# Second routing's logits from the old row and the activations, and the chain's steps in new slots

## The reference, cut to what matters

```
x = x + 0.5 * ffn(layernorm(x))          # 4096 rows of 128
x = x + attn(layernorm(x))               # a gated linear recurrence over time, then a gated FFN, then Wo
x = x + 0.5 * ffn(layernorm(x))

ffn(x):  gate_logits = x @ Wg            # 128 -> 12 experts
         topw, sel = top_k(gate_logits, 3); softmax over the three
         h = gelu(x @ Wup[e] + bup[e])   # 128 -> 512
         y = h @ Wdown[e] + bdown[e]     # 512 -> 128
         sum of the three chosen experts' y by weight
attn(x): u = silu(x@Wg + bg) * (x@Wi + bi); y = scan of u over time; y = Cp*y + Dp*u; normalise
         y = (silu(y@Wfg + bfg) * (y@Wfu + bfu)) @ Wfd + bfd; return y @ Wo + bo
```

## Time and profile before

| | us |
|---|---|
| median of 3 runs | 632.81 (632.74 to 634.7) |
| profiled execution, whole time | 633.43 |
| its span, first to last instruction | 631.7 |
| busy: TensorE / ScalarE / GpSimd / VectorE | 564.4 / 419.8 / 418.0 / 348.7 |
| first expert matmul | 43.6 |
| passes 1, 2, 3 begin (first up) | 171.5 / 320.0 / 473.3 |

### The profile page before, as it was taken

The page is one execution under the profiler, slowest core; times in us unless marked ns, Lnnn a source line. Parts: engine busy times, 40 slices in busy tenths (PEclk is TensorE's granted clock), DMA queues, the critical chain, the costliest instruction groups (busy, mean ns, idle before and its releaser), DMA issues.

```text
span 631.7 us, 17884 instructions
## 1 busy us (share of the span) xinstructions
PE 564.4 (89%) x4591; PEld 529.5 (84%) x4591; DVE 348.7 (55%) x1636; ACT 419.8 (66%) x1280; POOL 418.0 (66%) x432
## 2 busy tenths in 40 slices
PE   8469999999699999999999899999979999989505
PEld 7358999999699889879899789899979999989502
DVE  5983365371014688987727589888743532232206
ACT  2547686686366787887668688877657766656204
POOL 1137777777767775556677777066666777777774
PEclk9769999999799999999999999999999999999957
DMA  7577776789598786466478967466568888765137
GB/s 214 180 190 236 211 196 202 218 205 275 156 288 255 215 240 178 138 188 189 135 215 255 275 212 206 148 187 183 160 175 249 217 281 251 215 194 156 49 119 244
DMA packets 121847, 127.90 MB, mean 202 GB/s; under 512 B 17178, under 2 KB 84561, under 8 KB 121749
## 3 DMA queue, kind: packets, MB, share of 16 engines
q1 hardware_dynamic: 106452, 99.52, 53.2%
q0 software_dynamic: 12992, 26.11, 14.8%
q10 hardware_dynamic: 2304, 1.11, 0.6%
HBM read 96.62 MB, written 30.79 MB: 202 GB/s over the span
## 4 chain that ended last, share of the span: by engine, by line
PE 54%; DMA 13%; POOL 12%; DVE 10%; issue 8%; ACT 1%; SPq 0%; DVEq 0%; POOLq 0%; ACTq 0%
PE ps L931 20%; PE ps L944 20%; POOL YG L739 6%; DMA YG<-ys,SY 4%; POOL yk L750 3%; PE ps L799 3%; DMA xl<-xn,SG 3%; PE ps L825 2%; POOL xs L723 2%; PE ps L901 2%; DMA yk<-Ys,row 2%; DMA xs<-XN,SX 2%; PE ps L891 1%; DMA ys<-Ys 1%; DVE YG L1563 1%
## 5 line engine op out<-in xcount | busy, mean ns | idle before, releaser
L1097 ACT ACTIVATE hT<-ps,BU 128x128 f32<-128x128 f32 x944 | 269.4, 371 | 109.3 <-PE ps L931 106.7
L931 PE MATMUL ps<-xT,WU 128*128 128x128 f32 x1888 | 253.8, 278 | 4.2 <-ACT hT L1097 2.3
L944 PE MATMUL ps<-WD,hT 128*128 x1888 | 252.4, 277 | 4.8 <-DVE Ys L1635 3.7
L931 PEld LDWEIGHTS ps<-xT,WU 128*128 128x128 f32 x1888 | 233.4, 194 | 13.9 <-issue 13.9
L944 PEld LDWEIGHTS ps<-WD,hT 128*128 128x128 f32 x1888 | 231.7, 193 | 6.9 <-issue 6.8
L723 POOL DMA_INDIRECT xs<-XN,SX x144 | 144.5, 1004 | 87.6 <-issue 66.2
L739 POOL DMA_INDIRECT YG<-ys,SY x144 | 150.1, 1042 | 48.5 <-issue 40.6
L1635 DVE TENSOR_TENSOR Ys<-ps,BD 128x128 f32<-128x128 f32 x236 | 67.5, 289 | 193.4 <-PE ps L944 182.7
L708 POOL DMA_INDIRECT xl<-xn,SG x59 | 59.7, 1011 | 30.4 <-issue 14.0
L750 POOL DMA_INDIRECT yk<-Ys,row x59 | 59.0, 1000 | 18.0 <-issue 13.2
L1074 ACT ACTIVATE xT<-ps 128x512 f32<-128x512 f32 (+1 forms) x55 | 32.6, 593 | 6.6 <-PE ps L901 2.9
(11 more groups left out here) (255 smaller groups left out, 540.1 us busy)
## 6 DMA issues: line engine op xcount, KB each, us to landing
WU<-in_L_ffn_Wup_dram SPq DMA_DIRECT2D x236, 256.0 KB
ys<-Ys SPq DMA_DIRECT2D x42, 256.0 KB
xl<-xs SPq DMA_DIRECT2D x118, 66.0 KB, 3.0
xl<-xs SPq DMA_DIRECT2D x59, 64.0 KB, 1.9
WD<-in_L_ffn_Wdown_dram SPq DMA_DIRECT2D x12, 256.0 KB, 4.9
WD<-yk SPq DMA_DIRECT2D x4, 768.0 KB, 7.2
xs<-XN,SX POOLq DMA_INDIRECT x144
YG<-ys,SY POOLq DMA_INDIRECT x144
```

Source lines behind the costliest of these rows:

```text
L931: x = e.matmul(HB[i % 2][:, c * P:(c + 1) * P], WU[i % NW][:, c * P:(c + 1) * P], xT[m % 2][:, j * P:(j + 1) * P], start=True, stop=True)
L944: x = e.matmul(YB[i % 2][:, 0:D], hT[i % 3][:, c * P:(c + 1) * P], WDf[:, bass.ds(r + c * P, P)], start=(c == 0), stop=(c == C - 1))
L1097: x = e.activation(hT[i % 3][:, c * P:(c + 1) * P], HB[i % 2][:, c * P:(c + 1) * P], ACT.Gelu, bias=BU[:, bass.ds(b + c, 1)])
```

## The change

For the second routing the logits of the new row are made of three parts. The new row is x + y + bias, where y = tg times wfo. Its product with wgc is (old normalised row x wgc) x deviation of the old row, plus tg x (wfo wgc), plus (bias x wgc). G1 makes the first part from sT, which A1 has turned already, and adds the third; A7 makes the second part from tg right after its own products; L on VectorE adds them (lgn) and goes on as before. The step T, its copy and the product of the new row with wgc go, in CHAIN alone (pass 0's ROUTE keeps them). S1 adds a reciprocal (sd). W2 and W3, in pass 0, make wgk = [wfo wgc, bias wgc]; `bo` is loaded once more as a column. Nearly all slots of CHAIN are new, the first table steps A0 to A2 of pass 2 come two slots earlier, FETCHED has nothing for tiles 0 and 1, `load_rows` for the next pass comes one tile earlier, and in first() the aggregates and part of the deviation move between the chosen() steps.

```diff
-BIAS = [("V", "B3", 3), ("PA", "W0", 3), ("PAV", "W1", 5), ("S", "W1", 7)]
+BIAS = [("V", "B3", 3), ("PA", "W0", 3), ("PAV", "W1", 5), ("S", "W1", 7), ("PVA", "W2", 7), ("PV", "W3", 9)]
 CHAIN = [
-    ("V", "G0", (10, 17, 25, 30, 10, 17, 24, 30)),
-    ("V", "G2", (14, 20, 27, 34, 14, 20, 26, 32)),
-    ("V", "S1", (15, 21, 28, 36, 15, 20, 27, 33)),
-    ("A", "G", (17, 23, 29, 38, 17, 22, 28, 35)),
-    ("PA", "A1", (18, 24, 31, 39, 18, 23, 30, 36)),
-    ("PA", "A2", (18, 25, 34, 40, 18, 24, 33, 39)),
-    ("V", "C1", (18, 26, 35, 42, 18, 25, 33, 40)),
...
-    ("PV", "A7", (31, 38, 44, 52, 28, 36, 44, 50)),
-    ("PA", "T", (32, 39, 45, 53, 30, 38, 45, 51)),
-    ("V", "N", (32, 39, 44, 52, 30, 39, 45, 50)),
-    ("V", "N'", (33, 41, 44, 53, 32, 40, 45, 50)),
-    ("PV", "L", (33, 40, 47, 53, 32, 39, 46, 52)),
-    ("A", "N", (35, 42, 46, 54, 33, 41, 47, 53)),
-    ("PVG", "K", (35, 41, 49, 55, 35, 41, 48, 54)),
+    ("V", "G0", (9, 15, 21, 27, 11, 17, 21, 28)),
+    ("V", "G2", (14, 19, 25, 30, 14, 19, 25, 30)),
+    ("V", "S1", (15, 19, 26, 31, 15, 19, 25, 31)),
+    ("A", "G", (16, 21, 27, 32, 17, 21, 27, 33)),
+    ("PA", "A1", (17, 22, 28, 34, 18, 22, 29, 35)),
+    ("PA", "A2", (17, 23, 29, 36, 18, 23, 31, 37)),
+    ("P", "G1", (17, 23, 29, 37, 18, 23, 32, 37)),
+    ("V", "G1", (17, 23, 28, 42, 21, 23, 32, 47)),
+    ("V", "C1", (17, 23, 29, 36, 18, 23, 33, 37)),
...
+    ("PV", "A7", (31, 37, 44, 50, 29, 36, 43, 47)),
+    ("V", "N", (32, 40, 45, 50, 32, 39, 43, 47)),
+    ("V", "N'", (34, 40, 45, 50, 33, 39, 44, 49)),
+    ("V", "L", (33, 38, 44, 52, 30, 36, 45, 48)),
+    ("A", "N", (35, 41, 47, 53, 35, 41, 46, 53)),
+    ("PVG", "K", (35, 41, 46, 55, 32, 40, 47, 54)),
 ]
-TABLES_AT = ((34, 38), (50, 63), (51, 64))
+TABLES_AT = ((34, 38), (50, 63), (49, 64))
-FETCHED = tuple(min(K * NT, 6 + (13 * k) // 25) for k in range(NTL))
+FETCHED = tuple(min(K * NT, 6 + (13 * k) // 25) if k > 1 else 0 for k in range(NTL))
...
-                if n + 1 < NPH and k in (NTL - 3, NTL - 2):
-                    load_rows(NG * (n + 1) + k - (NTL - 3))
+                if n + 1 < NPH and k in (NTL - 4, NTL - 3):
+                    load_rows(NG * (n + 1) + k - (NTL - 4))
...
+                elif kind == "G1":
+                    e.wait_ge(s_e1, c)
+                    old = bank(step)
+                    for j in range(4):
+                        i = e.matmul(old[:, j * E:(j + 1) * E], sT[q][:, j * P:(j + 1) * P], wgc[:], start=True, stop=True)
+                    i.then_inc(s_g1, 1)
...
+                    new = bank(step, 1)
+                    for j in range(4):
+                        i = e.matmul(new[:, j * E:(j + 1) * E], tg[q][:, j * P:(j + 1) * P], wgk[:, 0:E], start=True, stop=True)
+                    i.then_inc(s_lg, 1)
...
+                    if p:
+                        new = psum[USED[("A7", h, q, p)][1][0]]
+                        e.wait_ge(s_dv, dv.n)
+                        e.tensor_tensor(lgn[:], new[:, 0:4 * E].rearrange("p (t e) -> p t e", e=E), lgo[q][:], ALU.add
+                                        ).then_inc(s_d2, 1)
...
+                    dv.on(e.reciprocal(sd[q][:], nr[q][:]))
+                elif kind == "G1":
+                    old = ps[0]
...
+                    e.tensor_tensor(
+                        lgo[q][:], old[:, 0:4 * E].rearrange("p (t e) -> p t e", e=E),
+                        sd[q][:, :].rearrange("p (t o) -> p t o", o=1).to_broadcast([P, 4, E]), ALU.mult).then_inc(s_d1, 1)
+                    e.wait_ge(s_d1, c)
+                    dv.on(e.tensor_tensor(
+                        lgo[q][:], lgo[q][:], wgk[:, E:2 * E].rearrange("p (o e) -> p o e", o=1).to_broadcast([P, 4, E]), ALU.add))
...
                 stats(0)
                 stats(1)
-                for q in range(NQ):
-                    chosen(q)
-                    if q + 2 < NQ:
-                        stats(q + 2)
+                stats(2)
+                chosen(0)
+                stats(3)
+                spread(0, NT // 2)
+                chosen(1)
+                spread(NT // 2, NT)
...
```

More of the change, by code:

```diff
@@ L343, in macaron_kernel @@
         BO3 = sb("BO3", [3, D], BF16)
-        wfdT, wfo = sb("wfdT", [P, D]), sb("wfo", [P, D])
+        wfdT, wfo, woT, bT = (sb(n, [P, D]) for n in ("wfdT", "wfo", "woT", "bT"))
+        wgk = sb("wgk", [P, 2 * E])
+        sd = [sb(f"sd{c}", [P, 4]) for c in range(NQ)]
+        lgo = [sb(f"lgo{c}", [P, 4, E]) for c in range(NQ)]
+        lgn = sb("lgn", [P, 4, E])
         sT, tg, ag = ([sb(f"{n}{c}", [P, 512]) for c in range(NQ)] for n in ("sT", "tg", "ag"))
@@ L425, in macaron_kernel @@
             "s_t4", "s_e4", "s_g5", "s_i5", "s_a5", "s_u5", "s_wp", "s_wt", "s_wo", "s_wb", "s_p7", "s_X"))
+        s_q2, s_q2c, s_q3, s_q3c, s_g1, s_d1, s_d2 = (sem(n) for n in ("s_q2", "s_q2c", "s_q3", "s_q3c", "s_g1", "s_d1", "s_d2"))
         s_fin, s_out, s_fs, s_fp, s_fe = (sem(n) for n in ("s_fin", "s_out", "s_fs", "s_fp", "s_fe"))
@@ L882, in side @@
                              skip_group_check=True).then_inc(s_wo, 1)
+                elif kind == "G1":
[4 more added lines that the diff above has]
+                    i.then_inc(s_g1, 1)
+                elif kind == "W2":
+                    w2 = bank(step)
+                    e.matmul(w2[:, 0:D], wat["Wo"][:], wfdT[:], start=True, stop=True)
+                    e.matmul(w2[:, D:D + 1], wat["Wo"][:], vec["bfd"][:, 0:1], start=True, stop=True,
+                             skip_group_check=True).then_inc(s_q2, 1)
+                elif kind == "W3":
+                    e.wait_ge(s_q2c, 2)
+                    w3 = bank(step)
+                    e.matmul(w3[:, 0:E], woT[:], wgc[:], start=True, stop=True)
+                    e.matmul(w3[:, E:2 * E], bT[:], wgc[:], start=True, stop=True, skip_group_check=True).then_inc(s_q3, 1)
                 elif kind == "A7":
                     e.wait_ge(s_u5, c)
+                    e.wait_ge(s_q3c, 1)
                     e.wait_ge(s_wb, 2)
@@ L1051, in side @@
                     e.activation(wfo[:], ps[0][:, 0:D], ACT.Copy, scale=0.5).then_inc(s_wb, 1)
+                elif kind == "W2":
+                    e.wait_ge(s_q2c, 1)
+                    e.activation(woT[:], ps[0][:, 0:D], ACT.Copy, scale=0.5).then_inc(s_q2c, 1)
                 elif kind == "TO":
@@ L1226, in side @@
                 elif kind == "L":
-                    lg = ps[0]
                     v = V[h][:, 4 * q:4 * q + 4, :]
                     e.wait_ge(s_lg, r)
+                    if p:
[3 more added lines that the diff above has]
+                                        ).then_inc(s_d2, 1)
+                        e.wait_ge(s_d2, c)
+                        lg = [lgn[:, j, :] for j in range(4)]
+                    else:
+                        lg = [ps[0][:, j * E:(j + 1) * E] for j in range(4)]
                     for j in range(4):
-                        i = e.max(v[:, j, :], lg[:, j * E:(j + 1) * E])
+                        i = e.max(v[:, j, :], lg[j])
                     dv.on(i)
@@ L1234, in side @@
                     for j in range(4):
[L1235 removed]
+                        i = e.max_index(IX[q][:, j, :], v[:, j, :], lg[j])
                     dv.on(i)
@@ L1288, in side @@
                     e.wait_ge(s_c1, 2 * c)
+                    e.wait_ge(s_g1, c)
                     dv.on(e.tensor_tensor_scan(sT[q][:], vec["A"][:, 0:1].to_broadcast([P, 512]), tg[q][:], 0.0,
@@ L1324, in side @@
                             e.wait_ge(s_bp, 2 * n + 2)
+                elif kind == "W2":
+                    e.wait_ge(s_q2, 1)
+                    e.tensor_tensor(bT[:], ps[0][:, D:D + 1].to_broadcast([P, D]), vec["bo"][:, 0:1].to_broadcast([P, D]), ALU.add
+                                    ).then_inc(s_q2c, 1)
+                elif kind == "W3":
+                    e.wait_ge(s_q3, 1)
+                    e.tensor_copy(wgk[:], ps[0][:, 0:2 * E]).then_inc(s_q3c, 1)
                 elif kind == "B3":
@@ L1466, in stats, with spread @@
                         dv.on(e.bn_stats(st16[:, 4 * q + j, :], X[:, 4 * q + j, :]))
+                def spread(a, b):
+                    e.wait_ge(s_dv, dv.n)
+                    for t in range(a, b):
+                        i = e.bn_aggr(mv16[:, t, :], st16[:, t, :])
+                    dv.on(i)
+                    e.wait_ge(s_dv, dv.n)
                 def chosen(q):
@@ L1482, in first @@
                 stats(1)
-                for q in range(NQ):
-                    chosen(q)
-                    if q + 2 < NQ:
-                        stats(q + 2)
+                stats(2)
[4 more added lines that the diff above has]
+                spread(NT // 2, NT)
+                dv.on(e.tensor_scalar(v16[:], mv16[:, :, 1], 1e-5, None, ALU.add))
+                e.wait_ge(s_dv, dv.n)
+                dv.on(e.tensor_scalar(nr16[:].bitcast(I32), v16[:].bitcast(I32), -0.5, RSQRT_SEED, ALU.mult, ALU.add))
+                e.wait_ge(s_dv, dv.n)
```

(11 more changed lines are left out.)

33 lines of the change are left out of this document (10 added, 23 removed), and 18 rows, old and new, of the table CHAIN.

## The result

The changed kernel is slower: median 640.0 us (637.72 to 644.75, four runs) against 633.75 us (632.74 to 634.72, four runs) of the kernel before on the same chip, ratio 1.0089, 95% interval 1.0054 to 1.0123 (the quotient of the two medians, 1.0099, lies in it; the sums below go by the ratio, +5.6 us). The forecast was 628.2 us with a range up to 633.3. The profiled execution took 641.01 us, its span 638.9. In the changed kernel an up product is L960, a down product L973, VectorE's output copy Ys L1703, G1's product L895, A7's new product L921.

A forecast was written before the change was run, and what follows sets the result against it. TensorE was taken to bound passes 1 and 2, GpSimd pass 3 from its start. Terms -1.5 + 3.0 - 0.9 - 2.3 - 3.0 = -4.7 us gave a median of 628.2 us, range 624 to 633.3.

The forecast's parts named there:

- The start: In first(), before pass 0: the counts' operation starts earlier and GpSimd's first gather moves with it, -1.5 us (bounds 0 and 1.6).
- TensorE per chunk: Passes 1 and 2: T and L go, G1 and A7's second half come, +0.38 us per chunk, +3.0 us for eight.
- rival E: Short products' weight loads hide behind neighbours, so a group costs only its streaming; eight chunks change by -3.1, 622 us; chance 0.02.
- The idle term: TensorE in passes 1 and 2: 2.4 us of waits go, 1.5 new ones come; net -0.9 us, bounds -4 and +8.4.
- K of the last chunk: Pass 2, slot 54: L and tables come earlier, so VectorE's K can go at about 461.1; -2.3 us, bounds 0 and -2.5.
- The turn: Pass 2 to 3: GpSimd's 3.28 us gap, a wait for the last ys store, goes; -3.0 us, bounds -1.0 and -3.3.
- its price of nothing: Turn to pass 3: TensorE's 2.88 us wait for rows should mostly go, worth nothing at the end as TensorE leads GpSimd.
- D: VectorE waits at G0 of chunk 2, slot 21, for gathers and holds TensorE, 8.4 us in two passes; 637.4 us; chance 0.09.
- "Wrong" signs: Profile signs against the forecast, among them gather waits, TensorE idle above 8 us in passes 1 and 2, GpSimd waiting for Ys.
- "Waits DVE from YG gathers": Sign against the forecast: VectorE waits of several us for gathers at G0 or G2.

The follow-up runs named there:

- the run with the start alone: Kernel before with only the new order of the first table in first(): ratio 0.9958 (0.9938 to 0.9979), -2.7 us.
- The doubled group: Changed kernel with G1's eight short product instructions issued twice per chunk: 1.017 (1.0128 to 1.0212) to the kernel before, 5.1 us above the changed kernel.
- The doubled VectorE operations: Changed kernel with VectorE's four added operations (reciprocal, product and two sums) issued twice per chunk: 1.0087 to the kernel before, 0.1 us below the changed kernel.
- the kernel with start and turn: Kernel before with first()'s new order, second tables at slot 49, no gathers after tiles 0 and 1, rows loaded a tile earlier: 0.9892, 627.18 us against 634.93.
- the spread kernel: Changed kernel with pass 1's row tables at slots 47 to 49 instead of 50 to 52, pass 2's last-chunk N' at 52 instead of 49: 1.0004 to the kernel before.
- logits alone: Kernel before with only the new way to the second logits, kept steps in old slots: 1.019, +12.1 us; on the 955.22 us chip 1.0013.

## Why the prediction was wrong

**The start** (-1.5 us) was right as far as pass 0: the first gather came at 37.69, forecast 38.0. At the turn from pass 0 to 1 the wait grew from 4.68 to 5.65 us and 0.6 us of it was left in the changed kernel's profile; the run with the start alone shows -2.7 us, interval -1.3 to -3.9. In the profile of that run TensorE keeps its 2.0 us through pass 1; why the changed kernel doesn't is open.

**TensorE per chunk** (+3.0 us) was right. By the rows from start to start, G1 and A7's new product take 3.32 and 3.25 us for four chunks of pass 1, and T and L took 1.91 and 3.35: +1.3, and +1.6 in pass 2 by the same count. TensorE's busy time rose by 2.3 us in pass 1 (147.58 less 145.31) and 2.8 in pass 2 (148.72 less 145.95), which also holds what waits and the lower clock cost it (below). The doubled group (0.64 us, and at least 0.2 with both intervals, where E has 0.04) rules out that such products hide behind their neighbours (rival E).

**The idle term** (-0.9 us, bounds -4 and +8.4) is the step that failed. In the two profiles TensorE's idle time in passes 1 and 2, without the turn to pass 3, went from 7.2 us (10.5 less 3.3) to 13.5 (14.4 less 0.9): +6.3 us. That lies inside the bounds, but the upper one came from gathers, another mechanism. I wrote that T, copy, L and their waits disappear and took back 2.4 us. I then put new waits at 1.5 us and looked for them at gathers alone. What came is another wait: TensorE for a free output bank while VectorE works through steps of one slot. Two places of it account for 5.4 us (2.6 either way), measured by taking them apart. The prediction had the pieces in hand: it put the tables at 49 to 51 and L at 48 in pass 2, said "VectorE can go at about 461.1", and counted VectorE's free time (44 to 50 us in a pass) as cover. Free time in a pass is no cover for one slot. The doubled VectorE operations, for which no cost shows, fit that from the other side: some 0.55 us more a chunk (102.54 and 113.28 us of VectorE in passes 1 and 2, 100.33 and 111.10 in the changed kernel) does no harm that could be measured.

**K of the last chunk** (-2.3) came out: from slot 54 to the first of the twelve scatters it is 4.3 us where it was 6.8, -2.5 us. VectorE's last K cast (474.38) is 1.6 us behind TensorE's K product (472.83), under the 2 us forecast. But this gain was bought by the packing of N' and A0 into slot 49, and N' at 52 shows that the packing wasn't needed for it: that kernel is 3.1 us faster. Either part of the change suffices for most of the gain: 1.8 us come with the earlier tables alone, 2.5 with the new chain and the tables in their old slots.

**The turn** (-3.0) came out in full, and alone start and turn bring -6.9 us, 2.4 more than my two terms. By the profiles GpSimd's pass 3 starts 6.9 us earlier there (476.88 for 483.77), in three parts: 2.1 that TensorE is early at slot 54, 1.8 from the K step, 3.0 from the gap. So the surplus over the two terms is mainly K's gain, which I had booked as a term of its own. TensorE's wait for rows at the turn has no part in it: it comes at 470.64, behind the first of the twelve scatters (465.33), so its price of nothing stands.

**The account of logits and slots.** From the kernel with start and turn to the changed one it is 12.5 us, where my terms (+3.0, -0.9, and the 0.5 of K's -2.3 that the earlier tables don't bring) give 1.6. Of the 12.5, 5.4 us are the two packed places (shown by experiment), and 3.0 are the products (rows, and the doubled group). K gives 0.7 back (5.0 us there, 4.3 here), so 4.8 are left. From the trace alone, not from an experiment: in the spread kernel TensorE runs at half the clock for three groups behind late rows in pass 2 (from 358.52 on, 1.31, 1.71 and 1.36 us from start to start where 0.90 is usual, +1.7; in the changed kernel two groups at 360.92 and 362.66, 1.74 and 1.71, +1.6), it waits about 2 us more in pass 2 than the kernel with start and turn alone (6.5 for 4.7), and 2 to 3 us are busy time that no group explains; part of it stands around waits (a group before a wait takes 1.06 us, else 0.90; the group behind one 0.97 to 0.99). Why the rows come late there (2.12 us for 0.66 before) is open.

**The rivals.** D, with 0.09, gave nearly the right time (637.4) by the wrong mechanism, so that was luck; the run with G0 alone put back refutes it. "Wrong" signs that I had named did show: idle time in passes 1 and 2 far above 8 us (5.7 and 8.7, of which 0.9 at the turn to pass 3). "Waits DVE from YG gathers" were four in the two passes, 5.0 us in all (before, five with 2.5), the longest 2.34 us, and they cost nothing measurable.

## What to carry to other kernels

An engine that copies results out of a double-buffered bank must come back every two tiles. What counts is each piece of other work between two copies against what the producing engine has to do meanwhile, and not the copier's free time in the pass. Here pieces of 4.36 and 4.49 us, with nothing but tiles of 1.79 us on TensorE beside them, held it up; pieces of 3.58 and 3.99 did not, nor one of 4.70 beside TensorE's own side steps, nor one of 7.20 in the kernel with start and turn alone (395.56 to 402.76), beside 3.0 us of them. When steps of a written-out order are moved, write down for each slot what the copying engine and the producing engine do in it, the tables included, before counting what the chain gains.

A change in several parts is to be timed part by part: here two parts of small edits brought 7 us and were hidden under a third that cost 12. The kernel with start and turn alone, 627.2 us, is faster than both.

## What the runs showed of the hardware that was not expected

One chip ran the same kernel in 955.22 us instead of 634, with TensorE at a mean clock of 0.81 to 0.82 and the other engines' busy times unchanged. The differences between kernels were much smaller there (logits alone +0.1% instead of +1.9%). Which chip a comparison runs on can decide what it shows.

A short wait can cost more than its length. Behind the 2.12 us wait at 360.28 the granted clock fell to the lower of its two levels (1.2 in place of 2.4 GHz; 0.51 of full speed from 361 to 364 us, 1.00 from 365 on), and two groups took another 1.6 us. Behind the 1.74 us wait at 315.88 it stayed at 1.00.

The Trainium skill ("TensorE: Matmul & The Clock Gate", "Back-to-back issue gap") gives about 60 cycles for a matmul of up to 64 columns; the run with G1 twice measured 0.64 us for eight such instructions, and the rows 0.81 to 0.90, where an estimate by that figure gives 0.2. The same section calls its formula one for isolated matmuls, which counts too little at few columns because it leaves out the weight load. So the figure was no price for this stream, and my prediction should not have weighed it as one; the measurement decides.
